# Attention scores of two heads side by side on TensorE's rows, from six products of bf16 parts, with the maxima's rows stored by two queues

## The chip, the cores and the metric

The kernel runs on one core of one Trainium2 chip. The metric is the device time of one execution in microseconds. Engines are named as in the profile: PE is TensorE, DVE is VectorE, ACT is ScalarE, POOL is GpSimd, SP is the queue of SyncE, which here issues DMAs only.

## The reference, cut to what matters

The program is two blocks on 2 x 1024 tokens of width 128: attention and a quantized feed-forward layer, then a scan and a mixture of experts. Only the attention is touched by the change:

```
B, T, D, H = (4, 256, 128, 16); HD = D // H        # the input here is (2, 1024, 128), HD = 8
q, k, v = (proj(Wq, bq), proj(Wk, bk), proj(Wv, bv))
q = q * cos + rotate_half(q) * sin
k = k * cos + rotate_half(k) * sin
attn = jnp.einsum('bhqd,bhkd->bhqk', q, k) * scale
attn = jax.nn.softmax(attn, axis=-1)
out = jnp.einsum('bhqk,bhkd->bhqd', attn, v)
return out @ Wo.T + bo
```

For each of 2 x 16 heads that is a score matrix of 1024 x 1024 over 8 channels, its row maxima, the exponential, and the product with the values.

## The kernel before, in words

**Parts.** q and k in float32 are each split into three bf16 parts (`PARTS = 3`), first, second and third, whose sum is nearly the float32 value. The eight pieces u (four chunks of 512 tokens, q and k of each, order `PIECES`) come from DVE (lines 1216 to 1222), their first part from ACT (L917), the rest from POOL (L830), the second from ACT (L910), the third from POOL (L823). SP stores them in DRAM (`q_dram`, `k_dram`, L604) and loads them back as stacks: `qs` and `ks` hold on the rows 0 to 71 all 3 x 3 pairs of parts of 8 channels, so that one matmul over these rows adds nine products of parts; the next two rows hold the maxima in `qs` (high and low bf16 part) and ones in `ks`; rows 74 to 95 are filled (`fill_set`, L567), so a matmul spans `ROWS = 96` rows. One stack holds one pass, that is four heads (`QUAD`), and there are three sets of buffers (`SETS`).

**Passes.** There are 8 passes (`PASSES`), each of 16 steps: two halves of 512 queries, in each 8 tiles of 128 keys. In a step PE computes for each of the four heads j the scores, turned, of 128 keys x 512 queries, already less the maxima (L1680; four matmuls, in the PSUM banks 4 to 6 in turn; each waits until the exponential three before it has been read, `s_exp`). ACT takes the exponential of each (L937). PE multiplies with the values for the step before (`products`, L1707).

**Maxima.** The maxima have to be there before the scores of a half are. They are computed from a product of fewer parts, 32 rows a head, on `qm` and `km` (`score_pair`, L1651, two matmuls a tile, each on its own 32 rows), or in the first pass from the stacks (`score_half`, L1640); DVE reduces each tile (L1240, L1237), two tiles a step. A pass has 32 such tiles, 16 in each half. The tiles run `LEAD = 22` ahead of the step's own pass. After 16 tiles DVE packs the 16 negated maxima of each query as high and low bf16 (L1247 to L1252), transposes them (L1255), and SP stores them in the rows of `qs` by four DMAs (`store_maxima`, L636). The first matmul of a half waits for these (`s_nrow`, L1670).

**Order.** Each engine runs its instructions in the order written. In a step PE's order is: scores of heads 0 and 1, the two tiles for maxima, scores of heads 2 and 3, products of the step before. POOL after its parts copies values (`values`, L837) and then waits for PE in each pass. SP goes through `one_pass`: store maxima, load `qm` and `km` of a later pass (`load_heads`, 24 DMAs a pass), store maxima, load the stacks.

Of the kernel before, what the change touches and what calls it, by code (L numbers as in the profile page):

```python
# [38 lines left out]
PROD = PARTS * PARTS * HD  # L39
ROWS = 96  # L40
# [32 lines left out]
def build_kernel(nc, i, out):  # L73
# [9 lines left out]
    with ctx:  # L83
# [50 lines left out]
        fill = sb("fill", [4 * (ROWS - PROD), 2, 2 * BANK], BF16)  # L134
        blank = fill[:, 0, 0:BANK]
        stacks = [[sb(f"{w}{n}", [ROWS, 2, QUAD, BANK], BF16) for w in ("qs", "ks")] for n in reversed(range(SETS))][::-1]
# [81 lines left out]
        q_dram = nc.dram_tensor("q_dram", (PASSES, 2, PARTS, QC, BANK), BF16, kind="Internal").ap()  # L218
        k_dram = nc.dram_tensor("k_dram", (PASSES, 2, PARTS, QC, BANK), BF16, kind="Internal").ap()
# [30 lines left out]
        s_fill = sem("s_fill")  # L250
# [8 lines left out]
        s_nrow = [sem(f"s_nrow{n}") for n in range(2)]  # L259
        s_st = sem("s_st")  # L260
# [103 lines left out]
        def part(u, n):  # L364

            return parts[:, u, n] if u < 6 else num_b[:, (PARTS * (u - 6) + n) * BANK:(PARTS * (u - 6) + n + 1) * BANK]

# [178 lines left out]
        LOADS = 16 * 2 * (PARTS + 1)  # L546
        HEAD_LOADS = 16 * 2 * 3 * QUAD

        @block.sync
        def _(sp):  # L550
# [47 lines left out]
            def store_parts(u, groups):  # L598

                c, kind = PIECES[u]  # L600
                sp.wait_ge(s_part3, u + 1)
                dst = (q_dram, k_dram)[kind]
                for g in groups:
                    sp.dma_start(dst[4 * (c // 2) + g, c % 2].rearrange("n c t -> c n t"),  # L604
                                 part_rows(u, slice(QC * g, QC * g + QC))).then_inc(s_parts_out[u], 16)
# [11 lines left out]
            def load_q(it, p, f, done):  # L617
                sp.dma_start(qs[p][0:PROD, f], q_dram[bass.ds(it, 1), f].rearrange(
                    "o n (d h) t -> (o n d) (h t)", h=QUAD).unsqueeze(1).to_broadcast([PARTS * HD, PARTS, QUAD * BANK])).then_inc(done, 16)

            def load_k(it, p, f, done):
                for a in range(PARTS):
                    sp.dma_start(ks[p][HD * PARTS * a:HD * PARTS * (a + 1), f], k_dram[bass.ds(it, 1), f].rearrange(
                        "o n (d h) t -> d (o n) (h t)", h=QUAD)).then_inc(done, 16)

            def load(it, p):

                for f in range(2):
                    load_q(it, p, f, s_qk[p])
                    load_k(it, p, f, s_qk[p])  # L630
# [29 lines left out]
            for u in range(CHUNKS):  # L660
                store_parts(u, (1,))
# [1424 lines left out]
```

## Time and profile before

| what | value |
|---|---|
| median of 3 runs | 906.85 us (905.33 to 908.17) |
| the profiled execution's own time | 907.05 us, its span 905.3 us |
| PE, DVE, ACT, POOL busy in the span | 86%, 88%, 76%, 27% |
| passes of the attention | from the first score matmul at 69.7 us to about 418.5 us |
| granted TensorE clock, mean | 0.94 |

The span is what lies between the first and the last instruction of the profiled execution. A busy share is that of the whole span, so it mixes the stages; the sections below look into one stage. A granted clock of 1.00 is 2.4 GHz, and 0.50 is 1.2 GHz.

### The profile page before, as it was taken

The page shows a single profiled execution, that of the slowest core. Times are in us where ns is not written, and L with a number is a line of the kernel's source. Part 1 is how long each engine was busy: PE and PEld are TensorE (multiplying, and loading weights), DVE is VectorE, ACT ScalarE, POOL GpSimd, SP SyncE. Part 2 cuts the span into 40 slices and gives each one's busy share as a digit, 9 for nine tenths or more (in the row PEclk, how much of TensorE's full clock was granted, in tenths as well). Part 3 has the DMA queues.
Part 4 walks back from the last instruction along what each step waited for, and adds up shares of the span by engine and source line. Part 5 has one row for each costly group of instructions (what it writes and reads, how often), then busy time and mean ns, then how long its engine had stood idle before and what let it go on. Part 6 is the DMA issues. An engine that isn't in the chain of part 4 may idle for free.

```text
span 905.3 us, 12616 instructions
## 1 busy us (share of the span) xinstructions
PE 779.2 (86%) x4297; PEld 414.1 (46%) x4312; DVE 794.6 (88%) x752; ACT 686.4 (76%) x1298; POOL 239.9 (27%) x136
## 2 busy tenths in 40 slices
PE   7789999999999999999666677677575899999998
PEld 3312222212122122225445556666575688888886
DVE  5998899998899899997997979999999887888765
ACT  2406888888788788886557799999998578888884
POOL 3800000000000000010001357898986701422000
PEclk9958999999999999999798788999998899999999
DMA  5313132312122220011001334565554202222101
GB/s 136 89 46 100 50 107 69 106 53 74 36 81 67 65 60 13 13 40 47 0 1 25 118 122 149 181 218 187 186 174 149 89 24 71 94 71 70 56 37 47
DMA packets 41467, 75.16 MB, mean 83 GB/s; under 512 B 7588, under 2 KB 25324, under 8 KB 40764
## 3 DMA queue, kind: packets, MB, share of 16 engines
q1 hardware_dynamic: 41404, 74.36, 26.0%
q8 instruction: 34, 0.56, 0.2%
q14 instruction: 29, 0.24, 0.1%
HBM read 64.71 MB, written 8.31 MB: 81 GB/s over the span
## 4 chain that ended last, share of the span: by engine, by line
PE 50%; DVE 27%; ACT 11%; issue 9%; POOL 2%; DMA 0%; DVEq 0%; ACTq 0%; POOLq 0%
PE ps L1680 9%; PE ps L1707 9%; DVE nmax_k L1240 7%; PE ps L1969 6%; PE ps L1970 6%; PE ps L1971 6%; ACT dtb L1075 5%; PE ps L1651 4%; DVE hst L1409 4%; DVE nmax L1237 3%; ACT abar L1049 2%; PE ps L1867 2%; PE ps L1913 2%; PE ps L1790 1%; ACT prob L937 1%
## 5 line engine op out<-in xcount | busy, mean ns | idle before, releaser
L937 ACT ACTIVATE prob<-ps 128x512 f32<-128x512 f32 x512 | 272.5, 599 | 90.4 <-PE ps L1680 88.4
L1240 DVE TENSOR_REDUCE nmax_k<-ps 128x2 f32<-128x1024 f32 x224 | 262.3, 1219 | 28.2 <-PE ps L1651 27.0
L1680 PE MATMUL ps<-qs,ks 96*128 96x512 bf16 x512 | 159.4, 387 | 3.9 <-ACT prob L937 2.6
L862 POOL TENSOR_TENSOR hc<-hst,cbr 128x1024 f32<-128x1024 f32 x63 | 151.2, 2422 | 43.3 <-DVE hst L1409 22.7
L1409 DVE TENSOR_TENSOR_SCAN hst<-abar,ps 128x1024 f32<-128x1024 f32 x64 | 142.8, 2272 | 4.4 <-issue 1.9
L1707 PE MATMUL ps<-prob,vq 128*16 128x512 f32 x1024 | 134.6, 597 | 0.1
L1523 DVE TENSOR_TENSOR act_l<-act_t,act_h 128x1024 fp32r<-128x1024 f32 x64 | 91.8, 1444 | 34.5 <-ACT act_h L1172 34.5
L1075 ACT ACTIVATE dtb<-dtxt,bt 128x128 f32<-128x128 f32 x352 | 107.4, 394 | 2.9 <-PE ps L1867 2.9
L1680 PEld LDWEIGHTS ps<-qs,ks 96*128 96x128 bf16 x512 | 34.0, 97 | 153.0 <-ACT prob L937 121.7
L1168 ACT ACTIVATE act_t<-ps,b1t 128x512 f32<-128x512 f32 x128 | 81.8, 681 | 25.3 <-PE ps L1971 25.2
L1867 PE MATMUL ps<-ident,dtb 128*128 128x128 f32 x352 | 54.6, 303 | 45.7 <-DVE hst L1409 37.2
L1651 PE MATMUL ps<-km,qm 32*128 32x512 bf16 x448 | 67.5, 385 | 8.3 <-DVE nmax_k L1240 7.5
L1913 PE MATMUL ps<-ident,hc 128*128 128x128 f32 x512 | 73.6, 293 | 0.6 <-DVE hc L1554 0.6
L1049 ACT ACTIVATE abar<-dt,a_neg 128x1024 f32<-128x1024 f32 x64 | 71.7, 1144 | 2.8 <-DVE hst L1409 2.7
L1172 ACT ACTIVATE act_h<-act_t 128x1024 fp32r<-128x1024 f32 x64 | 67.9, 1061 | 2.0
L1867 PEld LDWEIGHTS ps<-ident,dtb 128*128 128x128 f32 x352 | 43.8, 155 | 56.1 <-DVE hst L1409 45.7
L1913 PEld LDWEIGHTS ps<-ident,hc 128*128 128x128 f32 x512 | 65.9, 154 | 5.3 <-issue 1.8
L837 POOL COPY vq<-v 128x256 f32<-128x256 f32 x8 | 3.1, 399 | 242.1 <-PE ps L1707 242.1
L476 POOL TENSOR_SCALAR stat<-stat 128x8 f32<-128x8 f32 x8 | 3.3, 415 | 226.0 <-DVE stat L424 158.5
L1969 PE MATMUL ps<-act_h,w_l 128*128 128x512 f32 x128 | 50.4, 394 | 1.7 <-DVE act_l L1523 1.6
L1651 PEld LDWEIGHTS ps<-km,qm 32*128 32x128 bf16 x448 | 18.7, 91 | 71.8 <-DVE nmax_k L1240 38.9
L1969 PE MATMUL ps<-xh,w_l 128*128 128x512 f32 x128 | 50.5, 394 | 0.0
(221 smaller groups left out, 1125.1 us busy)
## 6 DMA issues: line engine op xcount, KB each, us to landing
cbr<-s_dram SPq DMA_DIRECT2D x64, 512.0 KB, 3.9
gate<-c_dram SPq DMA_DIRECT2D x5, 1024.0 KB, 4.7
qs<-q_dram SPq DMA_DIRECT2D x16, 288.0 KB
ks<-k_dram SPq DMA_DIRECT2D x48, 96.0 KB
o_dram<-o_sb SPq DMA_DIRECT2D x14, 256.0 KB, 2.4
gate<-c_dram SPq DMA_DIRECT2D x6, 512.0 KB, 4.0
wf<-in_L_ffn_w SPq DMA_DIRECT2D x8, 256.0 KB, 5.0
wfq<-in_L_ffn_w SPq DMA_DIRECT2D x8, 256.0 KB, 4.9
```

Of the source, the lines that this page charges most:

```text
L862: nc.gpsimd.tensor_tensor(hc[:, m % RING], hst[:, m % RING], cbr[:, m % RING], ALU.mult).then_inc(s_hc, 1)
L937: nc.scalar.activation(prob[:, n % 8], ps[:, 4 + (first + n) % 3], ACT.Exp, scale=ATT_SCALE).then_inc(s_exp, 1)
L1075: ins = nc.scalar.activation(dtb[:, t % 2, k], dtxt[:, b, k], ACT.Copy, scale=bt[:, b, k, n:n + 1])
L1240: nc.vector.tensor_reduce(nmax_k[:, half, kk, 2 * pair:2 * pair + 2, qt], ps[:, 2 * pair:2 * pair + 2, :], AX.X, ALU.max, negate=True).the ...
L1409: nc.vector.tensor_tensor_scan(hst[:, m % RING], abar[:, m % RING], inflow_ps(m).rearrange("p k t -> p (k t)"), 0.0, ALU.mult, ALU.add).th ...
L1523: nc.vector.tensor_tensor(act_l[:, m % 2, h:h + 2], act_t[:, m % 2, h:h + 2], act_h[:, m % 2, h:h + 2].bitcast(F32), ALU.subtract).then_in ...
L1651: mm = nc.tensor.matmul(ps[:, 2 * pair + n], qm[p][rows, half, qt * P:(qt + 1) * P], km[p][rows, kk, :], start=True, stop=True)
L1680: nc.tensor.matmul(ps[:, 4 + (first + n) % 3], ks[p][:, kt // 4, j, kt % 4 * P:(kt % 4 + 1) * P], qs[p][:, half, j, :], start=True, stop=T ...
L1707: mm = nc.tensor.matmul(ps[32 * j:32 * j + VW, 7], vq[p][:, kt, j, :], prob[:, (4 * s + j) % 8], start=(kt == 0), stop=(kt == KT - 1))
L1867: mm = nc.tensor.transpose(ps[:, 2 * (m % 2) + k // 4, k % 4 * P:(k % 4 + 1) * P], dtb[:, t % 2, k], ident[:])
L1913: mm = nc.tensor.matmul(ps[:, 6 + k // 4, k % 4 * P:(k % 4 + 1) * P], hc[:, m % RING, k * P:(k + 1) * P], ident[:], start=False, stop=(n = ...
L1969: nc.tensor.matmul(dst, w_l, r_h, start=start, stop=False)
```

## The change

Six of the nine products of parts are kept (`PAIRED`, pairs of q's and k's part), 48 rows, and with the two rows of maxima a head takes 50. Heads with an even number lie on the rows from 0 on, those with an odd number on the rows from 64 on (`side`), so a stack is 128 rows x 2 x 2 x 512. The parts are stored in DRAM once for each product in which they stand (`copy_to`, `first_copies`), so that a load is a plain copy. In `ks` the ones come from a memset of the whole tile on POOL in place of the DMA of `fill`. The maxima's columns are ordered so that one half of the transposed rows belongs to the even heads, the other to the odd ones: SP stores the first (`s_nrow`), POOL the second (`s_prow`). The second batch's parts are stored by POOL (`store_second_batch`) and no longer by SP.

```diff
+PAIRED = ((0, 2), (0, 0), (0, 1), (1, 0), (1, 1), (2, 0))
-PROD = PARTS * PARTS * HD
-ROWS = 96
+PROD = len(PAIRED) * HD
+ROWS = PROD + 2
+SIDE = 64
-        stacks = [[sb(f"{w}{n}", [ROWS, 2, QUAD, BANK], BF16) for w in ("qs", "ks")] for n in reversed(range(SETS))][::-1]
+        stacks = [[sb(f"{w}{n}", [P, 2, QUAD // 2, BANK], BF16) for w in ("qs", "ks")] for n in reversed(range(SETS))][::-1]
-        q_dram = nc.dram_tensor("q_dram", (PASSES, 2, PARTS, QC, BANK), BF16, kind="Internal").ap()
+        q_dram = nc.dram_tensor("q_dram", (PASSES, 2, len(PAIRED), QC, BANK), BF16, kind="Internal").ap()
+        def side(h, rows=ROWS):
+            return slice(SIDE * (h % 2), SIDE * (h % 2) + rows)
+        def maxima_rows(p, half, n, z):
+            return qs[p][SIDE * n + PROD:SIDE * n + ROWS, half].rearrange("r h (q t) -> r (h q) t", t=P)[:, :, 32 * z:32 * z + 32]
+        def copy_to(u, copy, groups):
+            c, kind = PIECES[u]
+            dst = (q_dram, k_dram)[kind][4 * (c // 2) + groups.start:4 * (c // 2) + groups.stop, c % 2, copy]
+            return dst, part_rows(u, slice(QC * groups.start, QC * groups.stop))[:, PAIRED[copy][kind]]
...
             def load_heads(it, p, f):
-                for h in range(QUAD):
-                    q, k = (t[bass.ds(it, 1), f].rearrange("o n (d h) t -> (o n d) h t", h=QUAD)[0:2 * HD, h]
-                            for t in (q_dram, k_dram))
-                    sp.dma_start(km[p][32 * h:32 * h + 32, f], k.unsqueeze(0).to_broadcast([2, 2 * HD, BANK])).then_inc(s_qm[p], 16)
-                    for a in range(2):
-                        sp.dma_start(qm[p][32 * h + 16 * a:32 * h + 16 * a + 16, f],
-                                     q[HD * a:HD * a + HD].unsqueeze(0).to_broadcast([2, HD, BANK])).then_inc(s_qm[p], 16)
+                for t, to in ((k_dram, km), (q_dram, qm)):
+                    sp.dma_start(to[p][:, f], t[it, f, 1:5].rearrange("n (d h) t -> h (n d) t", h=QUAD)).then_inc(s_qm[p], 16)
+            def load_stack(stack, dram, it, f, done):
+                for n in range(2):
+                    sp.dma_start(stack[side(n, PROD), f], dram[it, f].rearrange(
+                        "n (d h m) t -> m (n d) h t", d=HD, m=2)[n]).then_inc(done, 16)
...
             def store_maxima(it, p, half):
                 sp.wait_ge(s_nmax, 2 * it + half + 1)
                 for z in range(4):
-                    sp.dma_start(
-                        qs[p][PROD:PROD + 2, half].rearrange("n h (q t) -> n (h q) t", t=P)[:, :, 32 * z:32 * z + 32],
-                        nmax_t[32 * z:32 * z + 32, half, :]).then_inc(s_nrow[half], 16)
+                    sp.dma_start(maxima_rows(p, half, 0, z), nmax_t[32 * z:32 * z + 16, half, :]).then_inc(s_nrow[half], 16)
...
@@ gpsimd @@
+            def store_maxima(it, p, half):
+                pool.wait_ge(s_nmax, 2 * it + half + 1)
+                for z in range(4):
+                    pool.dma_start(maxima_rows(p, half, 1, z), nmax_t[32 * z + 16:32 * z + 32, half, :]).then_inc(s_prow[half], 16)
+            def store_second_batch(pieces):
+                for u in pieces:
...
+                    for copy in range(len(PAIRED)):
+                        pool.dma_start(*copy_to(u, copy, slice(0, QUAD))).then_inc(s_parts_out[u], 16)
...
             for p in range(SETS):
                 values(p, p)
-            with pool.Fori(1, PASSES // SETS) as r:
-                for p in range(SETS):
-                    pool.wait_ge(s_pv, STEPS * (SETS * (r - 1) + p + 1))
-                    values(SETS * r + p, p)
...
+            for n in range(1, SETS):
+                nc.gpsimd.memset(ks[n][:], 1.0).then_inc(s_set[n], 1)
+            store_second_batch(range(CHUNKS, 2 * CHUNKS))
+            store_maxima(0, 0, 0)
+            for it in range(PASSES):
+                store_maxima(it, it % SETS, 1)
+                if it + 1 < PASSES:
+                    store_maxima(it + 1, (it + 1) % SETS, 0)
+                if it + SETS < PASSES:
+                    pool.wait_ge(s_pv, STEPS * (it + 1))
+                    values(it + SETS, it % SETS)
...
@@ tensor, one_pass @@
                     if kt == 0:
                         pe.wait_ge(s_nrow[half], 64 * (it + 1))
+                        pe.wait_ge(s_prow[half], 64 * (it + 1))
...
-                        nc.tensor.matmul(ps[:, 4 + (first + n) % 3], ks[p][:, kt // 4, j, kt % 4 * P:(kt % 4 + 1) * P],
-                                         qs[p][:, half, j, :], start=True, stop=True).then_inc(s_st, 1)
+                        nc.tensor.matmul(ps[:, 4 + (first + n) % 3], ks[p][side(j), kt // 4, j // 2, kt % 4 * P:(kt % 4 + 1) * P],
+                                         qs[p][side(j), half, j // 2, :], start=True, stop=True).then_inc(s_st, 1)
```

POOL, at the end of the parts and before the passes. Before, the copies of the values follow the last third part, and after them POOL only waits for PE:

```order
L830 TENSOR_TENSOR rest<-rot,num 128x512
L823 TENSOR_TENSOR num<-rest,num 128x512 x2
L837 COPY vq<-v 128x32x8 x3
L843 UNCONDITIONAL_BRANCH
L837 COPY vq<-v 128x32x8 x3
```

With the change, in the same place:

```order
L832 TENSOR_TENSOR rest<-rot,num 128x512
L825 TENSOR_TENSOR num<-rest,num 128x512 x2
L839 COPY vq<-v 128x32x8 x3
L860 MEMSET ks 128x2048 x2
L854 DMA q_dram<-parts 4x32x512 x6
L854 DMA k_dram<-parts 4x32x512 x6
L854 DMA q_dram<-num 4x32x512 x6
L854 DMA k_dram<-num 4x32x512 x6
L846 DMA qs<-nmax_t 2x8x32 x12
L839 COPY vq<-v 128x32x8
```

Two memsets and 24 stores of parts now stand on POOL ahead of its first store of maxima.

PE, where the first pass begins (L1680 before and L1704 after are the scores, L1640 and L1663 the tiles for the maxima). Before:

```order
L1680 MATMUL ps<-qs,ks 128x512 [waits s_nrow0]
L1680 MATMUL ps<-qs,ks 128x512
L1640 MATMUL ps<-ks,qs 128x512 [waits s_max]
L1640 MATMUL ps<-ks,qs 128x512
```

And with the change:

```order
L1704 MATMUL ps<-qs,ks 128x512 [waits s_prow0,s_nrow0]
L1704 MATMUL ps<-qs,ks 128x512
L1663 MATMUL ps<-ks,qs 128x512 [waits s_max]
L1663 MATMUL ps<-ks,qs 128x512
```

The order on PE is the same; the first score matmul waits for one semaphore more, that of POOL's stores.

## Rows read from the trace of the kernel before

**Rows 1.** The page's head and the busy times of the engines.

```profile
span 905.3 us, 12616 instructions
PE 779.2 (86%) x4297; PEld 414.1 (46%) x4312; DVE 794.6 (88%) x752; ACT 686.4 (76%) x1298; POOL 239.9 (27%) x136
```

**Rows 2.** Groups by line: busy us, mean ns | idle before and its releaser.

```profile
L937 ACT ACTIVATE prob<-ps 128x512 f32<-128x512 f32 x512 | 272.5, 599 | 90.4 <-PE ps L1680 88.4
L1240 DVE TENSOR_REDUCE nmax_k<-ps 128x2 f32<-128x1024 f32 x224 | 262.3, 1219 | 28.2 <-PE ps L1651 27.0
...
L1651 PE MATMUL ps<-km,qm 32*128 32x512 bf16 x448 | 67.5, 385 | 8.3 <-DVE nmax_k L1240 7.5
...
L837 POOL COPY vq<-v 128x256 f32<-128x256 f32 x8 | 3.1, 399 | 242.1 <-PE ps L1707 242.1
```

**Rows 3.** Chain that ended last, 44 to 150 us: start, us, what.

```profile
41.81 1.60 DVE v L1201 x8
43.55 1.02 PE ps L1640 x2
44.59 18.84 DVE nmax L1237 x16
...
112.33 0.33 PE ps L1651 x4
...
119.59 0.54 PE ps L1680 x2
120.13 0.59 PE ps L1651 x4
120.72 0.54 PE ps L1680 x2
121.25 0.98 PE ps L1707 x8
```

**Rows 4.** The same chain at the end of a half, 366 to 372 us.

```profile
364.77 2.37 DVE nmax_k L1240 x2
367.17 0.19 DVE nmax L1247
...
368.00 2.25 DVE nmax_k L1240 x2
370.25 0.05 issue
370.30 0.39 PE ps L1651 x2
```

**Rows 5.** Source L1255, the transposes of the maxima: ns, first and last start us.

```profile
L1255 DVE STREAM_TRANSPOSE nmax_t<-nmax_p x16: 211/211/213, 64.0 to 389.3; 128x32 bf16<-128x32 bf16 x16
```

**Rows 6.** Source L1680, the score matmuls: ns, first and last start.

```profile
L1680 PE MATMUL ps<-qs,ks x512: 377/389/635, 69.7 to 418.1; 96*128 96x512 bf16 x171
```

**Rows 7.** Timeline, 193 to 201 us: start, us, engine, line.

```profile
193.80 0.21 DVE L1255 STREAM_TRANSPOSE nmax_t<-nmax_p 128x32 bf16<-128x32 bf16 x1
194.04 2.64 SPq L636 DMA_DIRECT2D qs<-nmax_t  x4
200.55 0.61 PE L1680 MATMUL ps<-qs,ks 96*128 96x512 bf16 x2
```

**Rows 8.** Timeline of POOL, 37 to 48 us, and its memsets at the start.

```profile
1.81 0.95 POOL L810 MEMSET fill<- 96x1024 bf16 x1
46.29 1.08 POOL L837 COPY vq<-v 128x256 f32<-128x256 f32 x3
```

**Rows 9.** Groups of POOL by line, 0 to 60 us.

```profile
L830 POOL TENSOR_TENSOR rest<-rot,parts 128x512 f32<-128x512 f32 x6 | 7.1, 1188 | 6.9 <-ACT parts L917 6.6
L477 POOL TENSOR_TENSOR stat<-stat,expo 128x8 f32<-128x8 f32 x2 | 3.3, 1648 | 0.2
```

**Rows 10.** Sources L604 and L636, SP's stores of parts and of maxima.

```profile
L604 SPq DMA_DIRECT2D q_dram<-parts x12: 344/435/513, 28.0 to 154.9; - x12
DMA to landing us min/median/max: 1.8/2.0/4.1
...
L636 SPq DMA_DIRECT2D qs<-nmax_t x64: 610/611/699, 64.2 to 391.5; - x64
```

**Rows 11.** Timeline of SP, 28 to 41 us.

```profile
33.31 0.30 SPq L604 DMA_DIRECT2D k_dram<-parts  x1
33.66 4.13 SPq L623 DMA_DIRECT2D ks<-k_dram  x6
```

**Rows 12.** Windows: busy us of PE, PEld, DVE, ACT, POOL, then clock, DMA share.

```profile
44.00:69.00 25.00, 21.20 (x43) 2.83 (x42) 24.20 (x24) 0.63 (x1) 3.37 (x6) 0.50 0.23 57
108.00:389.30 281.30, 271.73 (x1667) 56.86 (x1659) 252.73 (x261) 227.47 (x429) 2.00 (x5) 1.00 0.21 61
389.30:418.50 29.20, 25.73 (x152) 7.69 (x149) 28.13 (x32) 23.71 (x47) 3.33 (x2) 1.00 0.24 67
```

**Rows 13.** Chain that ended last, 389 to 411 us.

```profile
389.51 1.12 DVE num L1274
...
402.25 2.73 POOL stat L477
...
405.06 1.23 DVE xc L431
406.29 1.25 DVE wfq L537
```

More of the change, by code:

```diff
@@ L38 @@
 PARTS = 3
-PROD = PARTS * PARTS * HD
-ROWS = 96
+PAIRED = ((0, 2), (0, 0), (0, 1), (1, 0), (1, 1), (2, 0))
+COPIES = tuple(tuple(slice(r[0], r[-1] + 1, r[1] - r[0] if len(r) > 1 else 1) for r in
+                     ([n for n, pair in enumerate(PAIRED) if pair[kind] == part] for part in range(PARTS))) for kind in range(2))
+PROD = len(PAIRED) * HD
+ROWS = PROD + 2
+SIDE = 64
 ATT_SCALE = 1.0 / float(np.sqrt(np.float32(HD)))
@@ L259, in build_kernel @@
         s_nrow = [sem(f"s_nrow{n}") for n in range(2)]
+        s_prow = [sem(f"s_prow{n}") for n in range(2)]
         s_st = sem("s_st")
@@ L544, in build_kernel @@
         STORED = (slice(0, P), slice(0, 3 * P // 4))
[L546 to L547 removed]
+        LOADS = 16 * 2 * 2 * 2
+        HEAD_LOADS = 16 * 2 * 2
+        STORES = 16 * PARTS
         @block.sync
@@ L596, in load_scan_weights, with store_first, store_rest @@
                     sp.dma_start(wo_late[32 * j:32 * j + HD], wt[STORED[1].stop + HD * j:STORED[1].stop + HD * (j + 1), 5, :]).then_inc(s_wo, 16)
-            def store_parts(u, groups):
-                c, kind = PIECES[u]
+            def store_first(u, part):
+                sp.wait_ge((s_part1, s_part2, s_part3)[part], u + 1)
+                sp.dma_start(*first_copies(u, part)).then_inc(s_parts_out[u], 16)
+            def store_rest(u):
                 sp.wait_ge(s_part3, u + 1)
[L602 to L605, printed above, removed]
+                for copy in range(len(PAIRED)):
+                    sp.dma_start(*copy_to(u, copy, slice(1, QUAD))).then_inc(s_parts_out[u], 16)
@@ L808, in _ @@
             nc.gpsimd.memset(wo_late[:], 0.0)
-            nc.gpsimd.memset(fill[:, 0], 0.0)
-            nc.gpsimd.memset(fill[:, 1], 1.0).then_inc(s_fill, 1)
+            nc.gpsimd.memset(ks[0][:], 1.0).then_inc(s_set[0], 1)
             nc.gpsimd.memset(euler[:], float(np.exp(1.0)))
@@ L838, in values @@
                     "p o k (h d) -> p (o k) h d", d=HD)).then_inc(s_vq, 1)
+            def store_maxima(it, p, half):
[4 more added lines that the diff above has]
+                for u in pieces:
+                    pool.wait_ge(s_part1, u + 1)
+                    pool.wait_ge(s_part2, u + 1)
+                    pool.wait_ge(s_part3, u + 1)
+                    for copy in range(len(PAIRED)):
+                        pool.dma_start(*copy_to(u, copy, slice(0, QUAD))).then_inc(s_parts_out[u], 16)
             pool.wait_ge(s_v, 4)
@@ L1639, in score_half @@
                     pe.wait_ge(s_max, 32 * it + t - 1)
-                mm = nc.tensor.matmul(ps[:, 2 * (t % 2) + kk], qs[p][:, half, h, q * P:(q + 1) * P],
-                                      ks[p][:, kk, h, :], start=True, stop=True)
+                mm = nc.tensor.matmul(ps[:, 2 * (t % 2) + kk], qs[p][side(h, PROD), half, h // 2, q * P:(q + 1) * P],
+                                      ks[p][side(h, PROD), kk, h // 2, :], start=True, stop=True)
                 if kk == 1:
```

96 lines of the change are left out of this document (40 added, 56 removed).

## The prediction

> **What bounds the kernel now.** I read the page first [rows 1]: PE and DVE are both near nine tenths busy, which tells of no single bound. The groups by line narrow it to the attention [rows 2]: ACT idles 88 us waiting for the score matmuls, DVE 27 us for the products that it reduces. So in the passes both wait for PE, and PE in turn for them. The chain of waits shows how [rows 3]: a step on PE is two scores (0.54 us to the next work), the tiles for the maxima (0.33 us if all four matmuls start at once, 0.59 us where the second tile waits for DVE), two scores (0.54) and the products (0.98). The four matmuls of the tiles lie on four different groups of 32 rows and take less together than two scores on the same 96 rows.
>
> The step follows from that. Call the start of a step's first tile a. DVE can begin 0.39 + 0.05 us later [rows 4], reduces two tiles in 2.37 us, and only then, 0.05 us on, may the second tile of the next step start: a + 2.86. From there PE goes through 0.33 + 0.54 + 0.98 + 0.54 = 2.39 us to the first tile of the step after. So two steps take 5.25 us, one 2.62, and the 8 of a half 21.0 us. At the end of a half DVE spends 0.86 us on packing and turning the maxima (from 367.14 to 368.00 [rows 4]). Measured: from the first transpose to the last, 15 halves in 389.3 - 64.0 = 325.3 us [rows 5], 21.69 each. The loop through PE explains it, with 0.69 us for the end of a half. DVE alone would need 18.84 us for 16 reductions [rows 3] and 0.86, so 19.70.
>
> After the last transpose the chain is on DVE and POOL, with the work of the feed-forward layer [rows 13]. A faster score there gives nothing. All that can be won is won before 389.3 us.
>
> **The change part by part.** *Scores of two heads at once.* Heads 0 and 1 lie on rows 0 to 49 and 64 to 113, so they should start together as the tiles for the maxima do. I cost a pair of scores at 0.32 us, the 0.33 us of the four [rows 3], in place of 0.54; the bounds are these two. In the step twice 0.22 us fall away: 0.33 + 0.32 + 0.98 + 0.32 = 1.95, two steps 2.86 + 1.95 = 4.81, one 2.41, a half 19.2 + 0.69 = 19.9. DVE's own 19.70 is now almost the bound, so most of what PE gives beyond it would be lost anyway. I take 20.1, since the fourth score of a step still waits for the exponential three before it. That is 1.6 us for each of 15 halves, 24; the first half begins with PE at the slow clock (0.50 from 44 to 69 us [rows 12]) and has tiles of another kind, so I take 23 us. With DVE at its floor it would be 15 x 1.99 = 30, at 20.5 us a half 18.
>
> *Six products for nine.* A matmul's time does not follow its rows: 385 ns mean for 32 rows [rows 2] and 389 median for 96 [rows 6]. Fewer products cost or give nothing by themselves; they make the 50 rows possible.
>
> *The start.* SP issues more and smaller stores before the first load. But the last loads of `ks` before were issued from 33.66 to 37.8 us [rows 11], and PE began only at 43.55, behind DVE's bias of the values [rows 3]. A landing takes 2.0 us [rows 10], so there are 3.7 us of cover, and the new order (third part of the fourth piece, its store, then load) I put 0 to 2 us later. Cost nothing; if the cover went, it would cost what is over 3.7 us. In the passes SP has 20 DMAs less each; it is not waited for. POOL's memset of `ks` at the start takes twice one memset of `fill` [rows 8], as the two did. Nothing.
>
> *What now stands on POOL.* Its copies of values end at 46.29 + 1.08 = 47.4 us. Two memsets of 2048 columns at twice 0.95 us each [rows 8] bring it to 51.2. Then come 24 stores of parts and 4 of maxima, and behind them waits the first score matmul, which started at 69.7 us [rows 6]. The trace of before shows no DMA issued by POOL, so its price c has to be bounded. Below: what SP takes for such a store, 0.435 us [rows 10]. Above: what POOL takes for an operation of 128 x 512, 1.19 us, or for its slowest small one, 1.65 us [rows 9]. As the instruction stands on POOL, I go by a row of POOL's that only writes, the memset: c = 0.95 us. Then the last store of maxima starts at 51.2 + 27 x 0.95 = 76.9 and lands 2.0 us later, 78.9. The first score would be 9.2 us later than now. PE, and so ACT and DVE, have nothing else: the 22 tiles ahead are done by then. Loss 9 us. It vanishes if 51.2 + 27 c + 2.0 is under 69.7, so for c under 16.5 / 27 = 0.61 us.
>
> *The maxima by two queues.* Later halves have room: from the transpose to the first score that needs it are 200.55 - 193.80 = 6.75 us [rows 7], in the quicker steps about 6.1. SP's four DMAs take 2.64 us from 0.24 us after the transpose, and with the landing it is 4.9. POOL's would be 0.25 + 3 c + 2.0 = 5.1 us at c = 0.95. Neither is waited for; POOL's is from c = 1.28 on. So the second queue itself gives nothing: what it would shorten is covered already.
>
> One rule speaks against DMAs on POOL. The row first: POOL's small operation L477 takes 1.65 us at the start [rows 9], and 2.73 us at 402.25, where DVE works on SBUF beside it [rows 13]. The Trainium skill, page "SBUF — State Buffer", in the box on how DVE blocks DMA, says that a DMA issued from GpSimd has its descriptors written by that engine and is held up while VectorE runs a fast copy between SBUF tiles: 620 ns alone, 3100 ns under such a copy. By the first price the stall at the start would be 0.2 us and the sum 884; by the second the sum would be over 1000. No run here shows either, and while these DMAs are issued DVE mostly reduces from PSUM.
>
> **The sum**, against the profiled execution's own 907.05 us: -23 for the halves, +9 for POOL's queue at the start, 893. The median of the runs shown is 0.2 us lower, so 893 holds for it too. The clock was 1.00 in the passes and also in 389 to 418 us, where PE has no tiles to compute [rows 12], so I expect no fall from PE being idle a little more.
>
> **The rivals.**
> - *POOL's queue is quick*, c at or under 0.61 us: no stall, 884, and down to 881 if DVE comes nearer to its floor. For it: SP issues the same store in 0.435 us. Against: it is another engine, and each of its operations on so many rows takes near 1 us. Chance 0.25.
> - *The forecast*: c from 0.61 to 1.28 us, 884 to 902. Chance 0.48.
> - *POOL's DMAs are slow and slower*: from c = 1.28 us on, each half waits too. The 23 us are used up at c = 1.35: 27 x 1.35 - 16.5 = 20 us at the start and 15 x 0.2 = 3 in the halves. At 1.65 us [rows 9] it is 28 + 15 x 1.1 = 45 us of loss, 929. For it: POOL's slowing beside DVE [rows 13]. Against: DVE reads PSUM in these passes, and POOL's copies of the values, most of them beside these reductions, take 0.40 us in the mean [rows 2], near their 0.36 at the start [rows 8]. Chance 0.14. The rule of the Trainium skill quoted above would act by this mechanism.
> - *The pair of scores does not overlap*, because 50 rows on half of the array behave unlike 32 on a quarter, or the second waits for its bank: the change does not do what it says, a score pair stays at 0.54, and what is left is POOL's queue: 907 at c = 0.61, 916 at 0.95. Against: the tiles for the maxima overlap already. Chance 0.08.
> - *The start is late*: the chain of stores and loads through DRAM passes 43.5 us by more than its cover. It would add 2 to 4 us to any of these. Chance 0.05, 896.
>
> **How the numbers follow.** A measurement of this kernel tells about 0.3% from no change, 2.7 us. Below 904.1 lie the quick queue, nearly all of the forecast and the late start: 0.77. Within 0.3% (904.1 to 909.6) lie the upper end of the forecast's prices and a part of the two last losing cases: 0.07. Slower: 0.16. The likeliest is 893. The range takes in the quick queue at its best, 881, and the point where the slow queue uses up the gain, 907; what is left out is the slow queue beyond it and the case without overlap, 0.18.
>
> **What would show it.** In the profile of the changed kernel: two scores starting together, with about 0.32 us to PE's next work; transposes 20.1 us apart; ACT's and DVE's idle time behind PE down by more than half; POOL busy with DMAs from 51 us on, and the first score of the first pass at about 79 us with PE idle for 9 us before it; no PE wait for maxima at later halves. Scores that still take 0.61 us for two, one after the other [rows 7], halves of 21.7 us, or POOL's DMAs at under 0.6 or over 1.3 us would each make the prediction wrong, in the way that the rivals say.

## The result and the profile after

The changed kernel takes 928.66 us in the median of 4 runs (928.07 to 934.13), the kernel before beside it 906.09 (905.00 to 908.17): a ratio of 1.026, 95% interval 1.0216 to 1.0303. It is slower, by 22.6 us, where 893 was predicted and 907 was the upper end. One run of e11 and one of e12 below lay more than 1.5% above the fastest of its kernel, in a slower state, and is left out of the medians and ranges given.

The page's head and busy times of the changed kernel, against [rows 1]:

```profile
span 926.9 us, 12575 instructions
PE 748.8 (81%) x4297; PEld 403.2 (44%) x4312; DVE 793.5 (86%) x752; ACT 684.9 (74%) x1298; POOL 296.2 (32%) x225
```

PE does the same number of matmuls in 30 us less, and the span is 21.6 us longer. So the loss is idle time. The groups by line of the same page, against [rows 2]:

```profile
L957 ACT ACTIVATE prob<-ps 128x512 f32<-128x512 f32 x512 | 270.9, 599 | 116.9 <-PE ps L1704 116.1
L1260 DVE TENSOR_REDUCE nmax_k<-ps 128x2 f32<-128x1024 f32 x224 | 262.3, 1219 | 12.0 <-PE ps L1674 9.1
...
L1704 PE MATMUL ps<-qs,ks 50*128 50x512 bf16 x512 | 119.0, 394 | 40.4 <-DMA qs<-nmax_t 35.7
```

DVE waits for PE's tiles 9.1 us where it waited 27.0: the loop became shorter. ACT waits more, 116.9 for 90.4, and the last row says why: PE stood 35.7 us for a DMA of maxima. That is nearly all in one place. The source view of the transposes, against [rows 5], and windows of the stretches, against [rows 12] (busy us of PE, PEld, DVE, ACT, POOL, then the granted clock, the DMA share and GB/s):

```profile
L1278 DVE STREAM_TRANSPOSE nmax_t<-nmax_p x16: 211/211/213, 63.7 to 411.4; 128x32 bf16<-128x32 bf16 x16
```

The second of them, from the timeline:

```profile
123.75 0.21 DVE L1278 STREAM_TRANSPOSE nmax_t<-nmax_p 128x32 bf16<-128x32 bf16 x1
```

```profile
44.00:69.00 25.00, 21.17 (x43) 2.72 (x41) 24.49 (x24) 0.51 (x1) 25.00 (x35) 0.50 0.51 117
69.00:105.00 36.00, 0.56 (x2) 0.00 (x0) 1.82 (x2) 0.00 (x0) 0.36 (x1) 0.50 0.35 94
105.00:118.00 13.00, 12.40 (x45) 2.73 (x46) 7.06 (x6) 6.77 (x13) 0.00 (x0) 0.50 0.11 33
118.00:377.00 259.00, 241.99 (x1612) 55.29 (x1610) 245.18 (x254) 219.05 (x416) 30.94 (x57) 0.99 0.18 52
```

The first transpose is at 63.7 us as before (64.0). From 69 to 105 us next to nothing computes. The second transpose comes 60.1 us after the first, where it came 21.8 us after; the 14 halves from the second to the last take 287.67 us for 303.52; what follows the last takes 515.43 for 515.95. The account is -0.3 for the first transpose, +38.3 for the first half, -15.9 for the other halves and -0.5 for what follows, together +21.6 us.

The chain of waits of the changed kernel names the queue (SPq is a DMA instruction held on SP, DMA the transfer that was waited for; steps called issue, of at most 0.05 us, are left out here):

```profile
46.34 2.76 SPq L627
...
61.23 4.28 SPq L627
...
67.17 6.77 SPq L627
...
87.96 8.12 DMA q_dram<-parts
96.16 0.62 SPq L632
...
98.52 0.71 SPq L649
...
100.65 4.60 DMA qs<-nmax_t
105.30 0.60 PE ps L1704
```

L627 is the store in `store_rest`: SP's 24 stores of the parts of groups 1 to 3, each `[3, 32, 512]` in DRAM. SP then waits for their landing, loads the heads for the next pass (L632), and only then comes to its first store of maxima (L649), on which PE waits. The source view of these stores and of POOL's (L854 the second batch, L846 maxima; ns min/median/max, first and last start):

```profile
L627 SPq DMA_DIRECT2D q_dram<-parts x12: 656/1052/1690, 39.8 to 88.0; - x12
L627 SPq DMA_DIRECT2D k_dram<-parts x12: 906/3056/6772, 44.8 to 78.0; - x12
```

```profile
L854 POOL DMA_DIRECT2D k_dram<-parts x6: 691/691/691, 54.9 to 58.3; - x6
...
DMA to landing us min/median/max: 5.2/9.3/17.6
```

```profile
L846 POOL DMA_DIRECT2D qs<-nmax_t x64: 561/563/572, 67.1 to 413.6; - x64
...
DMA to landing us min/median/max: 1.7/1.7/16.0
```

SP's stores hold it for 0.66 to 6.8 us each, where the stores before held it 0.435 [rows 10]; all 24 together last from 39.8 to 89.2 us. POOL's cost it 0.69 us each, less than I had assumed, but they land 5 to 18 us later. The first maxima, issued behind them, land 9.4 to 16.0 us after their issue, later ones mostly after 1.7.

### The profile page after: what moved, and what is told of

Same layout as the page of the kernel before. It is cut to its first block, busy times and chain, and to the rows that moved or that the text cites. A ratio compares the mean times of both kernels' runs of the same rounds, so it can differ in the third digit from the quotient of the medians.

```text
span 926.9 us, 12575 instructions
## 1 busy us (share of the span) xinstructions
PE 748.8 (81%) x4297; PEld 403.2 (44%) x4312; DVE 793.5 (86%) x752; ACT 684.9 (74%) x1298; POOL 296.2 (32%) x225
## 4 chain that ended last, share of the span: by engine, by line
PE 43%; DVE 25%; ACT 13%; issue 10%; SPq 5%; POOL 2%; DMA 2%; DVEq 0%; ACTq 0%; POOLq 0%
DVE nmax_k L1260 9%; PE ps L1731 7%; PE ps L1993 6%; PE ps L1994 6%; PE ps L1995 6%; ACT dtb L1095 5%; PE ps L1704 5%; SPq L627 4%; PE ps L1674 4%; DVE hst L1432 4%; ACT abar L1069 3%; PE ps L1891 2%; PE ps L1937 1%; PE ps L1790 1%; PE ps L1865 1%
## 5 line engine op out<-in xcount | busy, mean ns | idle before, releaser
L957 ACT ACTIVATE prob<-ps 128x512 f32<-128x512 f32 x512 | 270.9, 599 | 116.9 <-PE ps L1704 116.1
L1704 PE MATMUL ps<-qs,ks 50*128 50x512 bf16 x512 | 119.0, 394 | 40.4 <-DMA qs<-nmax_t 35.7
L1731 PE MATMUL ps<-prob,vq 128*16 128x512 f32 x1024 | 137.1, 607 | 0.1
L846 POOL DMA_DIRECT2D qs<-nmax_t x64 | 35.6, 563 | 276.2 <-DVE nmax_t L1278 275.8
L1704 PEld LDWEIGHTS ps<-qs,ks 50*128 50x128 bf16 x512 | 31.2, 93 | 190.1 <-ACT prob L957 116.6
L1674 PE MATMUL ps<-km,qm 32*128 32x512 bf16 x448 | 82.5, 386 | 16.7 <-DVE nmax_k L1260 12.3
L1257 DVE TENSOR_REDUCE nmax<-ps 128x1 f32<-128x1024 f32 x32 | 37.6, 1218 | 41.8 <-PE ps L1663 41.7
L1937 PE MATMUL ps<-ident,hc 128*128 128x128 f32 x512 | 70.0, 283 | 0.6 <-DVE hc L1577 0.6
L1891 PEld LDWEIGHTS ps<-ident,dtb 128*128 128x128 f32 x352 | 41.8, 151 | 60.4 <-DVE hst L1432 53.4
L1937 PEld LDWEIGHTS ps<-ident,hc 128*128 128x128 f32 x512 | 62.3, 148 | 4.3 <-DVE hc L1577 0.9
L1674 PEld LDWEIGHTS ps<-km,qm 32*128 32x128 bf16 x448 | 20.7, 91 | 71.7 <-DVE nmax_k L1260 49.1
L1993 PE MATMUL ps<-act_h,w_l 128*128 128x512 f32 x128 | 50.4, 394 | 1.6 <-DVE act_l L1546 1.6
```

Of the source, the lines that this page charges most:

```text
L957: nc.scalar.activation(prob[:, n % 8], ps[:, 4 + (first + n) % 3], ACT.Exp, scale=ATT_SCALE).then_inc(s_exp, 1)
L1674: mm = nc.tensor.matmul(ps[:, 2 * pair + n], qm[p][rows, half, qt * P:(qt + 1) * P], km[p][rows, kk, :], start=True, stop=True)
L1704: nc.tensor.matmul(ps[:, 4 + (first + n) % 3], ks[p][side(j), kt // 4, j // 2, kt % 4 * P:(kt % 4 + 1) * P], qs[p][side(j), half, j // 2, ...
L1731: mm = nc.tensor.matmul(ps[32 * j:32 * j + VW, 7], vq[p][:, kt, j, :], prob[:, (4 * s + j) % 8], start=(kt == 0), stop=(kt == KT - 1))
L1891: mm = nc.tensor.transpose(ps[:, 2 * (m % 2) + k // 4, k % 4 * P:(k % 4 + 1) * P], dtb[:, t % 2, k], ident[:])
L1937: mm = nc.tensor.matmul(ps[:, 6 + k // 4, k % 4 * P:(k % 4 + 1) * P], hc[:, m % RING, k * P:(k + 1) * P], ident[:], start=False, stop=(n = ...
```

## The experiments

Two theories stood for the 36 us. **Shape**: SP's stores are slow because their outermost dimension in DRAM has 3 rows. **POOL**: they are slow because POOL's 24 stores are in flight at the same time. Each predicts that its own cure is enough. All ratios below are to the kernel before, run beside each kernel.

**e1_sp_shape.** `store_rest` writes a part's copies of one group at a time, 36 DMAs whose outer dimension is 32, in place of 24 with 3. POOL's order stays.

```diff
-                for copy in range(len(PAIRED)):
-                    sp.dma_start(*copy_to(u, copy, slice(1, QUAD))).then_inc(s_parts_out[u], 16)
+                for g in range(1, QUAD):
+                    for part in range(PARTS):
+                        sp.dma_start(*first_copies(u, part, g)).then_inc(s_parts_out[u], 16)
```

> Edit: SP's stores of groups 1 to 3 go out as 36 DMAs with 32 rows outermost, as those of before, in place of 24 with the 3 groups outermost; POOL's order is left. Shape theory (the outermost size of 3 keeps each store on few of the DMA engines, and SP's queue backs up behind them): each of the 36 takes 0.43 us, SP is through at 39.9 + 15.5 = 55 us, loads the heads by 60 and stores the maxima at 64; the first score then waits for POOL's stores alone and starts at 72 to 80 us (they are issued from 67 us and their landing behind the 24 stores is unknown). Time 895 to 903. Contention theory (POOL's 24 software-issued stores take the engines from SP's): SP's stores still stretch to beyond 75 us, the first score starts after 90, time over 912.

Measured: 917.07 us (915.13 to 919.25), ratio 1.0106 (1.007 to 1.0141). The first score starts at 91.5 us for 105.3. Source view of SP's stores:

```profile
L628 SPq DMA_DIRECT2D q_dram<-parts x18: 422/508/4295, 40.1 to 72.9; - x18
L628 SPq DMA_DIRECT2D k_dram<-parts x18: 422/429/528, 44.5 to 52.6; - x18
```

Up to 52 us, when POOL's stores (from 50.4 us on) have only begun, they take 0.43 us; behind, up to 4.3, and they end at 75.5 us. The first score is still 22.8 us later than in e3_both below, where that of the changed kernel is 36.6 us later: shape alone is not the cause. All three marks of the contention theory came true (stores beyond 75 us, first score after 90, time over 912).

**e2_pool_later.** POOL's second batch goes behind its first store of maxima; SP's stores keep their shape.

```diff
-            store_second_batch(range(CHUNKS, 2 * CHUNKS))
             store_maxima(0, 0, 0)
+            store_second_batch(range(CHUNKS, 2 * CHUNKS))
```

> Edit: POOL stores the second batch after its first store of maxima, not before; SP's stores keep the three groups outermost. Shape theory: SP's stores take about 1.3 us each whatever POOL does, 39.9 + 24 x 1.3 = 71 us, with the landing and the loads of heads the maxima's rows go out at about 77 and the first score starts at 81; time about 904. Contention theory: without POOL's stores SP's take 0.43 to 0.7 us, end by 57, the first score starts at 69.5 to 70, time about 892.

Measured: 930.33 us (923.98 to 933.63), ratio 1.0225 (1.0169 to 1.0281); first score at 105.05 us. Source view:

```profile
L627 SPq DMA_DIRECT2D q_dram<-parts x12: 656/1180/5511, 40.3 to 72.0; - x12
L627 SPq DMA_DIRECT2D k_dram<-parts x12: 1229/1345/2882, 45.2 to 62.8; - x12
```

POOL issued no DMA before 64 us, and still the stores to `k_dram`, all in that time, took 1.35 us in the median for e1's 0.43. So the shape is slow by itself. Then POOL's late stores, from 66.5 us on, met the rest of them: the last one of SP held it 5.5 us, SP waited for landings until 93 us, and the stall stayed whole. Both theories in their simple form fall; each cure leaves the other cause. (The shape theory had the 1.3 us a store right, but expected the first score at 81 us.)

Windows show what the shape does. The figure before the last is the mean busy share of the core's 16 DMA engines. First this kernel while SP stores `[3, 32, 512]`, then the kernel before the change while SP stores the second batch with 32 rows outermost:

```profile
52.00:60.00 8.00, 6.95 (x15) 0.90 (x14) 8.00 (x8) 0.00 (x0) 0.00 (x0) 0.50 0.20 66
```

```profile
155.00:161.00 6.00, 5.93 (x41) 1.24 (x38) 5.03 (x5) 4.93 (x10) 0.40 (x1) 1.00 0.91 205
```

A share of 0.20 is as much as 3.2 of the 16 engines busy, and 0.91 as much as 14.6. By an estimate from this, the 96 KB of a store take 1.5 us at the 66 GB/s of the first window, about the 1.35 us for which one holds SP.

**e3_both.** The two edits together.

> Edit: both, SP's stores with 32 rows outermost and POOL's second batch behind its first store of maxima. Either theory: no stall, the first score at 69.5 to 70 us as before, halves of 20.3 us as in the changed kernel, time 906 - 0.3 x 0 - (325.3 - 15 x 20.5) = 889, between 886 and 893. If the time is over 897 a third cause is open.

Measured: 899.63 us (896.34 to 902.99), ratio 0.9916 (0.9887 to 0.9945): below the changed kernel, and 0.8% below the kernel before, a small gain but clear of the interval. The first score starts at 68.71 us. Source view:

```profile
L628 SPq DMA_DIRECT2D q_dram<-parts x18: 424/429/617, 39.4 to 56.2; - x18
L628 SPq DMA_DIRECT2D k_dram<-parts x18: 423/429/430, 44.0 to 52.0; - x18
```

SP's stores end at 56.6 us. The stall is gone, and with it 36.6 us up to the first score. But the time is above what I expected (886 to 893, with a third cause open from 897 on). The first half takes 26.25 us, where it took 21.8 before; e10 and e11 ask why.

**e4_same_rows.** e3_both with odd and even heads on the same rows 0 to 49, so that no two score matmuls can overlap; the number of instructions, their columns and the DMAs are the same.

```diff
-    stacks = [[sb(f"{w}{n}", [P, 2, QUAD // 2, BANK], BF16) ...
+    stacks = [[sb(f"{w}{n}", [ROWS, 2, 2, QUAD // 2, BANK], BF16) ...
-    ... ks[p][side(j), kt // 4, j // 2, ...], qs[p][side(j), half, j // 2, :]
+    ... ks[p][:, kt // 4, j % 2, j // 2, ...], qs[p][:, half, j % 2, j // 2, :]
```

> Edit: the third kernel, but both heads of a pair lie on rows 0 to 49, so that their score matmuls can not run at once; all DMAs, sizes and orders are the same. If the gain of the passes is the overlap of two score matmuls: two scores take 0.61 us again, halves are 21.6 to 21.7 us, time 905 to 908. If it comes from elsewhere (fewer rows, SP's fewer DMAs, the loads): time stays under 897.

Measured: 1103.53 us (1101.50 to 1103.85), ratio 1.2148. This was far off. The halves take 34.5 us. A window, and the end of a step in the chain of waits:

```profile
108.00:370.00 262.00, 262.00 (x976) 30.81 (x974) 148.57 (x150) 136.10 (x252) 17.14 (x32) 0.50 0.11 33
```

```profile
241.12 0.96 PE ps L1705 x2
242.09 1.84 PE ps L1732 x8
```

In this window PE is busy without a gap, as it is from 80 to 588 us, and its granted clock is 0.50 (1.2 GHz) from 45 to 588 us. Products take 1.84 us for 0.98 [rows 3]. So this kernel could not tell the worth of the overlap; it showed another effect.

**e5_padded_rows.** e4_same_rows with every matmul on the stacks over 96 rows: rows 50 to 95 hold 0 in `qs` and 1 in `ks`, so they add nothing. One memset a set, that of `qs`, is new on POOL.

```diff
+            nc.gpsimd.memset(qs[0][:], 0.0)
-    ... qs[p][0:PROD, half, h % 2, h // 2, ...], ks[p][0:PROD, kk, h % 2, h // 2, :]
+    ... qs[p][:, half, h % 2, h // 2, ...], ks[p][:, kk, h % 2, h // 2, :]
```

> The kernel with both heads on the same 50 rows (e4_same_rows) again, but every matmul on the stacks goes over 96 rows, as in the kernel before: rows 50 to 95 are filled with 0 (queries) and 1 (keys), so that they add nothing. The instructions, their columns, waits and DMAs are those of e4_same_rows; two memsets of a stack a set are added on POOL. Theory A: the number of rows that a matmul goes over decides whether the full clock is granted in the passes. Then the granted clock is 1.00 from about 75 to 90 us on, the halves take 21.7 us as in the kernel before, and the time is that of e3_both and 15 x 1.15 us, 908 to 920. Theory B: the clock of 0.5 came from something else in e4_same_rows (its late start, the order of the heads, the smaller products): then it stays at 0.5, halves 34.5 us, about 1100.

Measured: 914.50 us (913.00 to 917.64), ratio 1.0078 (1.0054 to 1.0102). The same window:

```profile
108.00:370.00 262.00, 252.62 (x1536) 52.49 (x1534) 234.00 (x241) 210.51 (x397) 28.63 (x53) 0.99 0.17 49
```

The clock was back at 74 us, and 189 us are regained by rows that add nothing. The undisturbed halves (two lengths that recur in turn; a few others are up to 2.5 us longer) take 21.38 and 21.90 us as before the change (21.38 and 21.84), against 20.08 and 20.61 in e3_both: the overlap is worth 1.30 us a half. Theory A holds: the rows that the matmuls go over changed the granted clock.

**e6_full_rows_ahead.** e3_both with a zero matmul over 128 rows behind each of the tiles 8 to 21 ahead of the first pass.

> e3_both with one more matmul of zeros on all 128 rows (512 columns, into the bank of the products, which nothing else uses yet) behind each of the tiles 8 to 21 ahead of the first pass: 14 matmuls. PE was about 0.84 busy there (44 to 70 us) and DVE sets the pace at 1.19 us a tile. Theory A (the start of the first pass ran at the low clock because the tiles use 50 rows of 128): the granted clock is 1.00 before 75 us, the first half takes 21.5 to 22.5 us in place of 26.25, and the time is 4 to 5 us under e3_both, 894 to 897. Rival B (the low clock until 87 us has another cause, such as waits behind the first exponentials): T0 to T1 stays at 26 us, the time is that of e3_both or up to 2 us more (tiles of 1.29 us in place of 1.19).

Measured: 898.46 us (896.40 to 904.76), ratio 0.9909 (0.9878 to 0.994). PE was full from 60 to 75 us, and yet the clock stayed at 0.50 until 87 us as in e3_both:

```profile
60.00:75.00 15.00, 15.00 (x34) 2.54 (x34) 12.60 (x13) 0.30 (x1) 8.11 (x13) 0.50 0.31 75
```

So filling PE ahead of the pass did not bring it back; the first half again took 26.26 us. The tiles became late by 2.6 us (first transpose at 66.4), as rival B said. Its time is that of e3_both.

**e7_one_queue.** e3_both with all eight DMAs of maxima on SP.

> e3_both with all eight DMAs of maxima on SP, the second four behind the first four; POOL only stores the second batch. By the prediction's numbers the last lands 0.24 + 8 x 0.62 + 2.0 = 7.2 us after the transpose, and the first score that needs it starts 6.5 us after it in e3_both: 0.7 us more at each of 15 halves, 10 us over e3_both, if PE's wait is lost in full; at most 3 us if the step has room. So the second queue, which I had priced at nothing, would be worth 3 to 10 us in this layout. Rival: landings are quicker than 2.0 us and nothing is waited for: same as e3_both within 1 us.

Measured: 916.87 us (914.06 to 922.78), ratio 1.0098 (1.0065 to 1.0131), 17 us over e3_both, and 20 over e12_both_again, the same kernel on the chip of this run. In an undisturbed half the price is next to nothing: 20.15 us for 20.08. Nearly the whole loss is in three places. From 257.5 to 285.9 us a half takes 28.39 us for 20.59. The chain there (L616 and L637 are loads, L650 SP's stores of maxima, behind them four more):

```profile
257.47 0.62 SPq L637
...
262.61 0.68 SPq L650
...
264.68 1.62 DMA qs<-nmax_t
266.30 2.71 issue
269.01 0.61 PE ps L1705 x2
```

The transpose was done at 257.5, SP came to its eight stores 5.1 us later, and the last four were issued until 267.9. In e3_both POOL has these four away while SP still loads. Behind the wait the clock was 0.50 from 269 to 279 us. The first half takes 30.7 us, since SP's stores met POOL's batch (up to 3.5 us each). And behind the last transpose 526.7 us pass for 516.7: eight stores of 0.61 us stand ahead of the load of the denominators, DVE gets these late, and PE waits and falls to 0.50 from 409 to 429 us. I had expected a small loss in each half and found none there.

**e8_second_batch_on_sp.** e3_both with the second batch's 24 stores on SP in the second pass, still of the shape `[4, 32, 512]`.

> e3_both with the 24 stores of the second batch on SP in the second pass, as in the kernel before; POOL issues only maxima. Theory A (after e3_both's edits POOL's stores stand beside nothing that is waited for, and the slow first half is the clock): T0 to T1 stays at 26 us, time within 1.5 us of e3_both; SP's 24 stores take 24 x 0.44 = 10.6 us in the second pass, which may hold a load of heads but no maxima. Rival B (the stores of POOL from 66.7 to 83 us, on the DMA engines beside the loads of the next pass, delay the first half): T0 to T1 falls by 2 us or more.

Measured: 920.05 us (916.37 to 920.57), ratio 1.0114 (1.0089 to 1.014). The first half is unchanged, 26.36 us, so POOL's stores beside it don't slow it (rival B falls). But one later half takes 45.5 us, and theory A had no such loss. Source view of these stores, at a time when POOL issues none:

```profile
L731 SPq DMA_DIRECT2D q_dram<-parts x6: 536/554/929, 154.6 to 157.6; - x6
L731 SPq DMA_DIRECT2D k_dram<-parts x6: 1181/1328/1556, 158.6 to 165.5; - x6
```

After the first few, each holds SP 1.3 us, and the last lands 7.8 us after it was issued. My expectation of 0.44 us each was wrong: it is the shape again, now with no store of POOL's beside it. The window has a DMA share of 0.28, as much as 4.5 of 16 engines:

```profile
160.00:180.00 20.00, 17.30 (x120) 3.84 (x112) 18.38 (x20) 16.03 (x31) 2.63 (x5) 1.00 0.28 93
```

The maxima wait behind them.

**e9_pool_row_stores.** e1_sp_shape with POOL's batch over 32 rows too: 48 DMAs, still ahead of POOL's first maxima.

> e1_sp_shape (SP's stores of groups 1 to 3 as 36 DMAs of 32 rows) with POOL's second batch in that shape too: 48 DMAs over 32 rows in place of 24 over 4 x 32, still ahead of its first maxima. To be read from it is what happens to SP's stores while POOL's are issued: in e1_sp_shape they went from 0.44 to a mean of 1.45 us. Theory A (POOL's stores are slow to be worked off because of their 4 outer rows, and SP's wait behind them): SP's stay under 0.6 us in the mean and end before 60 us. Rival B (any stream of stores from POOL holds SP's up): their mean is again over 1 us and they end after 70 us. The time itself is worse either way, since 48 x 0.57 to 0.69 us on POOL end at 78 to 84 us and its maxima land at 83 us or later: first score at 83 to 90 us, 910 to 920.

Measured: 905.63 us (900.88 to 907.58), ratio 0.9958 (0.9938 to 0.9977), under the 910 to 920 expected, since POOL needed less for a store than I had assumed. Source view of SP's stores, and the timeline of PE's first score:

```profile
L628 SPq DMA_DIRECT2D q_dram<-parts x18: 423/430/783, 38.8 to 57.8; - x18
L628 SPq DMA_DIRECT2D k_dram<-parts x18: 423/429/1904, 43.5 to 53.1; - x18
```

```profile
75.88 2.26 POOL L847 DMA_DIRECT2D qs<-nmax_t  x4
...
79.39 0.61 PE L1706 MATMUL ps<-qs,ks 50*128 50x512 bf16 x2 [9.88 <-DMA qs<-nmax_t]
```

Theory A holds: from POOL's first store (50.45 us) on, none of SP's takes over 0.67 us, where e1 had up to 4.3; the longest above, 1.9 us, lies ahead of it. They end at 58.4 us (75.5 in e1). Twice as many stores cost POOL 0.54 us each, and its maxima now land 1.2 us after the last is issued. PE waits 9.88 us for POOL's queue, and the first half takes 36.15 us for e3_both's 26.25.

**e10_full_rows_between, e11_four_full_rows, e12_both_again.** e3_both with zero matmuls over 128 rows ahead of each pair of scores, in the first five steps (10 of them) or the first two (4); e12_both_again is e3_both once more, beside e11.

```diff
+                        if it == 0 and s < 5 and j % 2 == 0:
+                            nc.tensor.matmul(ps[:, 4 + (first + n) % 3], none_b[:, 0:1].to_broadcast([P, P]),
+                                             ks[0][:, 0, 0], start=True, stop=True)
```

> e3_both with ten more matmuls of zeros on all 128 rows (512 columns each), two in each of the first five steps of the first pass, one ahead of each pair of scores and into the same bank (the score then overwrites it). These are the steps in which the tiles for the maxima still go over 48 rows, and in which the granted clock was 0.50 (until 87 us; 73 us in the kernel before, where tiles and scores go over 96). Theory A (what a matmul goes over in rows brings the clock back): the clock is 1.00 at 73 to 78 us, the steps cost 0.2 us a zero matmul more after that, and T0 to T1 falls from 26.25 to 22 to 24.5 us; time 2 to 4 us under e3_both. Rival B (the clock comes back at 87 us whatever fills PE, as in e6_full_rows_ahead): ten matmuls at 0.43 us are added to a stretch that PE bounds, T0 to T1 is 29 to 31 us, time 3 to 4 us over e3_both.

> e10_full_rows_between with the zero matmuls in the first two steps only, 4 in place of 10; in that kernel the clock came back at about 77 us, behind six of them, and the last four ran in a stretch that the full clock had reached. Theory A (the few matmuls over 128 rows ahead of the third step are enough): clock 1.00 by 80 us, T0 to T1 24 to 25.5 us, time 1 to 2 us under e3_both. Rival B (the clock needs the rows of the later ones too): it comes back at 83 to 87 us, T0 to T1 is 26.5 to 28 us, time 0 to 2 us over e3_both.

> The kernel of e3_both again, on the chip of e11_four_full_rows, so that the two stand side by side: 896 to 901 us, ratio 0.985 to 0.995, T0 to T1 26.2 us. Rival: its gain on the kernel before was of one chip alone, ratio over 0.997.

Measured: e10 895.30 us (894.10 to 900.75), ratio 0.9868 (0.9845 to 0.9892); e11 899.23 (894.56 to 905.49), 0.9897 (0.9851 to 0.9943); e12 897.16 (892.44 to 902.27), 0.9901 (0.9872 to 0.9931). Windows from 75 to 80 us of e3_both and then of e10, the clock after POOL's busy time:

```profile
75.00:80.00 5.00, 5.00 (x21) 1.02 (x24) 2.85 (x4) 2.60 (x5) 5.00 (x8) 0.50 0.82 192
```

```profile
75.00:80.00 5.00, 5.00 (x22) 1.00 (x21) 2.50 (x3) 2.17 (x4) 5.00 (x9) 0.71 0.81 190
```

The clock returned at about 78 us in e10 and 80 in e11, and at 87 and 83 in the two runs of e3_both. That is the way theory A has it, but the two traces of one kernel lie 4 us apart, so it is supported and not shown; and it pays little. In e10 the zero matmuls use up what the clock gives: 25.8 us for the first half, between the two theories (22 to 24.5, and 29 to 31). In e11 the first half takes 24.5 us (24.6 in e12 without any, where 26.2 was expected), and the second 28.3 for 20.5. There the chain has:

```profile
88.54 0.66 SPq L650
...
89.24 2.32 SPq L650
...
92.46 4.84 DMA qs<-nmax_t
...
97.34 0.61 PE ps L1708
```

The second maxima, ready at 88.5 us instead of e3's 90.2, meet POOL's batch, issued until about 83 us, of which the last six land 10.7 us later in the median. e5 shows the same (86.9 us, half of 27.1). But in e12 they were ready at 88.5 us too, and its second half took 20.7 us; its batch had landed at 93.8 us, that of e11 at 95.6. What decides between the two is not shown. Of e3, e6, e10, e11 and e12 none can be told from another: the intervals overlap.

## Why the prediction was wrong

- **The failed step is "The start ... Cost nothing"**, for the stores behind the first loads. I priced what SP issues ahead of the first load, and had nothing for `store_rest`, the 24 stores between those loads and SP's first maxima. In the kernel before only the four stores of group 1 stood there; those of the groups 2 and 3 came behind these maxima. No run puts that order back. At the 0.435 us of [rows 10] they would end at 50 us. They ended at 89.2, since that row was for DMAs whose outermost dimension is 32 and these have 3. The first maxima on SP left at 98.5 us. e3_both undoes this together with POOL's batch and gives the two one number: 36.6 us to the first score, which the sum had at nothing for SP and at 9 for POOL.
- The Trainium skill, page "DMA: Bandwidth & Descriptors", section "Why a DMA increments its semaphore by 16 and not by 1", says that the number of engines of a DMA is the largest up to 16 that divides the slowest dimension of both sides. By that, 96 KB in `[3, 32, 512]` go to 3 engines and `[4, 32, 512]` to 4, in place of 16, as an estimate. The traces agree: the DMA share is that of 3.2 engines in e2 and of 4.5 in e8 (other DMAs run beside them), and of 14.6 in the kernel before; SP is held 1.35 us in e2 and 1.33 in e8, for 0.43 in e1. I had not weighed this rule.
- **POOL's queue ahead of its maxima**: the mechanism is right, both sizes were off. c measured 0.69 us for a store and 0.56 for maxima, not 0.95; the landing at the start was up to 16.0 us, not 2.0. The errors partly cancel, by luck: the last maxima were issued from 68.8 to 69.4 us and landed at 84.8, where 78.9 was forecast. PE did not feel it, since SP was later still. e9 shows a stall of the predicted kind alone: 52 DMAs of 0.54 us from 50.4 us, PE's wait 9.88 us, 9 forecast. That it comes so near is luck too, with twice the stores at little over half the price. My rule "no stall for c under 0.61" would hold only with a landing of 2 us.
- **The pair of scores**: right. Two start together and PE goes on after 0.32 us, so the rival without overlap falls; here a step of the timeline after:

```profile
160.59 0.39 PE L1704 MATMUL ps<-qs,ks 50*128 50x512 bf16 x2
160.91 0.82 PE L1674 MATMUL ps<-km,qm 32*128 32x512 bf16 x4
```

- **A half**: mis-sized. The undisturbed halves went from 21.38 and 21.84 us to 20.08 and 20.61, in the mean 21.61 to 20.34; the forecast was 21.7 to 20.1. The gain is 1.27 us, 1.30 in e5 against e3, not 1.6; over the 14 halves from the second on, with the disturbed ones, 15.9 us, where 22 were due. Part of it is that I took 21.69 as the start, the mean with the disturbed halves, for 21.61. The rest is in the pairs. In each of the halves from 144 to 226 us 13 of the 16 pairs start together, or within 0.03 us, and the second score of the other three comes 0.12 to 0.29 us late, 0.5 to 0.7 us a half, where I had allowed 0.2 (19.9 to 20.1). Each time it is the fourth score of a step, and it starts 0.05 to 0.06 us behind the end of the exponential three before it: the wait that I had named, priced too low. Such a pair in the timeline (PEld is the load of the weights for its second score):

```profile
174.65 0.67 PE L1704 MATMUL ps<-qs,ks 50*128 50x512 bf16 x2
174.93 0.09 PEld L1704 LDWEIGHTS ps<-qs,ks 50*128 50x128 bf16 x1 [0.19 <-ACT prob L957]
```

- **Six products "cost or give nothing by themselves"**: right for the matmul (median 386 ns against 389), wrong for the kernel. On the same side alone they cost 189 us by the clock (e4 against e5). Side by side in the passes the clock is 0.99. But in the first steps, where the tiles go over 48 rows of one side, it came back at 87 us (83 in e12) and not at 73. PE had no idle time at this clock from 75 to 80 us, and the first half took 4.5 us longer than before (2.8 in e12). I take the clock for the cause; e6, e10 and e11 do not prove it.
- **The second queue "gives nothing"**: right for the usual half (0.07 us in e7), wrong for the kernel: 17 to 20 us, where SP's queue is full of loads or its eight stores stand ahead of a load.
- **POOL's DMAs beside DVE**: the 64 stores of maxima cost 561 to 572 ns each, so the rule of the Trainium skill that I weighed (page "SBUF — State Buffer", the box on how DVE blocks DMA; the two prices stand below it, in the section "A bandwidth-pool intuition that's wrong (but worth ruling out)") was not seen to act. DVE mostly reduces from PSUM there; no run tried a copy in SBUF beside them.
- **The rivals**: "POOL's DMAs are slow and slower" gave 929 us, close to what was measured, by a mechanism that did not occur: c is 0.68 us in the mean, and no later half waits for maxima. "The start is late" did not occur either: the first transpose is at 63.7 us, 64.0 before.

With the stall removed, 899.6 and 897.2 us are what the change gave here (e3, e12): -15.7 us in the 14 halves, +4.5 (+2.8) in the first, and the rest within the spread. That is 4 to 7 us above my 893, and 9 to 12 under the kernel before.

## What to carry to other kernels

A price per DMA holds for the shape of the row that it was read from: look at the outermost dimension on both sides before it is used for another, and price every DMA that stands on the queue ahead of the one that is waited for. When a stall has two causes, undoing either alone can show little (here 14 and 0 of 37 us), so run both together before a theory is dropped. Work taken off TensorE's rows can take its clock too, and a second queue for a small transfer is worth most where the first is full.

## What was not expected of the hardware

- A store of 96 rows as `[3, 32, 512]` holds SP 0.7 to 6.8 us, the same rows stored with 32 outermost 0.43 us (the changed kernel, e3). POOL's cost per DMA does not show its queue: 0.69 us each, flat, while they landed 5.2 to 17.6 us later.
- Whether one queue disturbs the other depends on the shape: beside POOL's stores over 4 outer rows those of SP rise to 4.3 us, beside POOL's over 32 they stay at or under 0.67 (e1, e9).
- PE without a gap at a granted clock of 0.50 for over 500 us, with matmuls over 50, 32 and 128 rows; with 96 in place of 50 rows, and all else equal on PE, 0.99 (e4, e5). e6, where 14 matmuls over 128 rows ahead of the pass did not bring the clock back and ten between the scores did (e10), leaves open what brings it back.
